# Score and numerator banks exchanged, and layer norm, the head turns and v's projection at other places of a two-layer attention and expert step

## What is computed

```python
x = x + tanh(g_xattn[0]) * xattn0(layernorm(x), ctx, ctx)      # causal mask, 16 heads
x = x + tanh(g_ffn[0])   * moe0(layernorm(x))                  # 8 experts 256->256, top 2, and one shared expert
x = x + tanh(g_xattn[1]) * xattn1(layernorm(x), ctx, ctx)      # masked by length, 16 heads
x = x + tanh(g_ffn[1])   * moe1(layernorm(x))                  # 8 experts 256->1024, top 2

# xattn: q = x @ Wq.T, k = ctx @ Wk.T, v = ctx @ Wv.T
#        probs = softmax(q k^T / 4 + mask);  out = (probs @ v) @ Wo.T
```

## Time and profile before

| | us |
|---|---|
| median of three runs (1742.0, 1742.06, 1753.56) | 1742.06 |
| the profiled execution | 1747.6 |
| its span, first to last instruction | 1745.9 |
| PE busy, DVE busy, ACT busy, POOL busy | 1392.2, 1112.2, 793.0, 727.3 |

### The profile page before, as it was taken

One profiled execution on the slowest core, in us unless ns is written; L12 is line 12 of the kernel. 1 busy time (PEld: TensorE's weight loads), 2 busy tenths in 40 slices (PEclk: granted clock), 3 DMA queues, 4 the chain that ended last, 5 costly groups with the idle time before them and its releaser, 6 DMA issues. The chain is left out here.

```text
span 1745.9 us, 39897 instructions
## 1 busy us (share of the span) xinstructions
PE 1392.2 (80%) x12001; PEld 1176.9 (67%) x12002; DVE 1112.2 (64%) x3589; ACT 793.0 (45%) x1744; POOL 727.3 (42%) x630
## 2 busy tenths in 40 slices
PE   3798988888872777735888887878736999999997
PEld 3576767677651677734556555655426999999997
DVE  4588787877663455523788888887645555555543
ACT  2354545555430555532455455554422544544543
POOL 4334444444231366643344444443232344445422
PEclk9899999999985899975899999999977999999998
DMA  2333334333216677651333333332263324334322
GB/s 88 100 97 100 103 93 110 100 98 88 80 44 185 130 122 131 103 98 55 102 106 102 110 99 109 99 106 65 66 181 105 89 45 96 90 90 96 91 42 42
DMA packets 213629, 168.26 MB, mean 96 GB/s; under 512 B 21462, under 2 KB 207096, under 8 KB 213240
## 3 DMA queue, kind: packets, MB, share of 16 engines
q1 hardware_dynamic: 181112, 126.05, 26.3%
q0 software_dynamic: 26880, 35.80, 12.1%
q10 hardware_dynamic: 5504, 4.75, 1.0%
HBM read 63.80 MB, written 51.56 MB: 66 GB/s over the span
## 5 line engine op out<-in xcount | busy, mean ns | idle before, releaser
L1806 POOL DMA_INDIRECT out_rows<-e_y,e_token x68 | 110.5, 1625 | 235.6 <-DVE e_y L1862 215.8
L1888 ACT ACTIVATE e_h<-e_h,t_up_bias 128x256 f32<-128x256 f32 x272 | 110.5, 444 | 209.0 <-PE e_h L1924 209.0
L938 DVE TENSOR_REDUCE a_row_max<-a_scores 128x2 f32<-128x512 f32 x256 | 170.7, 680 | 41.5 <-PE a_scores L1579 39.9
L1268 ACT ACTIVATE s_w_rows<-a_scores_t 128x384 f32<-128x384 f32 (+1 forms) x256 | 137.7, 547 | 109.9 <-PE a_scores_t L1597 59.9
L1268 ACT ACTIVATE a_probs<-a_scores_t 128x384 f32<-128x384 f32 (+1 forms) x256 | 136.0, 546 | 108.0 <-PE a_scores_t L1597 58.3
L771 POOL DMA_INDIRECT routed_rows_dram<-r_rows,r_slot x128 | 128.3, 1003 | 94.0 <-issue 60.5
L1939 PE MATMUL e_y_bank<-e_down_hi,e_hidden_hi 128*128 128x256 f32 x544 | 157.9, 290 | 3.2 <-DVE e_hidden_lo L1835 3.2
L1924 PE MATMUL e_h<-e_xs_hi,e_up_hi 128*128 128x256 f32 x544 | 154.6, 284 | 3.7 <-DVE e_xs_lo L1827 3.5
L2097 POOL DMA_INDIRECT x_mid_dram<-l_y,l_token x76 | 119.0, 1565 | 86.7 <-ACT l_token L2191 48.5
L1924 PE MATMUL e_h<-e_xs_lo,e_up_hi 128*128 128x256 f32 x544 | 153.8, 283 | 0.0
L1939 PE MATMUL e_y_bank<-s_k_stack,e_hidden_hi 128*128 128x256 f32 x544 | 153.6, 282 | 0.0
(11 more groups left out here) (288 smaller groups left out, 4450.3 us busy)
## 6 DMA issues: line engine op xcount, KB each, us to landing
s_q_stack<-a_parts SPq DMA_DIRECT2D x384, 64.0 KB
s_k_stack<-a_parts SPq DMA_DIRECT2D x384, 64.0 KB
l_xs_rows<-routed_rows_dram SPq DMA_DIRECT2D x42, 258.0 KB
e_xs_rows<-routed_rows_dram SPq DMA_DIRECT2D x36, 258.0 KB
a_ctx_rows<-in_ctx SPq DMA_DIRECT2D x32, 256.0 KB, 3.2
t_up<-in_L_ffn_W SPq DMA_DIRECT2D x8, 1024.0 KB
t_down<-in_L_ffn_W SPq DMA_DIRECT2D x8, 1024.0 KB
routed_rows_dram<-pad_rows ACTq DMA_DIRECT2D x16, 258.0 KB, 9.9
```

Of the source, the lines that this page charges most:

```text
L938: nc.vector.reduce_max(row_max[:, :, h], bank[:].rearrange("p (c t) -> p c t", c=TC), AX_X).then_inc(maxed, 1)
L1268: nc.scalar.activation(probs[h % NP][:, 0:width], scores_t[h % 2][:, 0:width], ACT.Exp).then_inc(probs_ready, 1)
L1806: pool.indirect_dma_start(out=x_acc, out_offset=bass.IndirectOffsetOnAxis(ap=token[p][:, c:c + 1], axis=0), in_=y[p][:, c, :], in_offset=N ...
L1888: nc.scalar.activation(out, h_bank[g][:, at:at + TS], act_func, bias=routed.up_bias[:, bass.ds(e * FC + fc, 1)]).then_inc(hidden_ready, 1)
```

## The change

It does five things.

1. `SB = 3` score banks instead of two: `score_head` waits for the maxima of head h-3. The bank comes from the numerators: one `pv` bank. `mix_group` g=0 and g=2 therefore wait for the `turn_heads` just before, not for the one of an item earlier.
2. Layer norm on DVE: `ln_apply` goes from h=14 to the head of the next step (it is item `i+3` there), `ln_stats` from h=11 to the head of the step, `ln_mean` from h=12 to h=3. POOL's addition of the output bias to x (`bias_of`, layer zero alone) goes from the end of `rstd_of` to the head of POOL's next step.
3. The turning of the heads: `turn_heads` m=0 from h=14 to h=11, `scale_heads` from h=15 to 12, `turn_back` from 15 to 13. Of m=1, `turn_heads` stays at the head, `scale_heads` and `turn_back` go behind the maxima of heads 1 and 2.
4. `project_v` from h=6 to h=11, behind the ranks, with a wait for `counted`; `turn_ctx` from 12 to 13, its `turned_lo` on DVE from 13 to 14. v is copied out of PSUM on ACT in both layers (before: DVE in layer one).
5. `index_to_float` and `mark_chosen` from h=6 to h=8 in layer one (`MARK_AT`); in layer zero they stay at 5.

```diff
+    SB = 3
...
-        scores = [ctx.enter_context(nc.psum_tensor(f"a{layer}_scores{n}", [P, 512], F32)) for n in range(2)]
+        scores = [ctx.enter_context(nc.psum_tensor(f"a{layer}_scores{n}", [P, 512], F32)) for n in range(SB)]
...
-        pv = [ctx.enter_context(nc.psum_tensor(f"a{layer}_pv{n}", [P, 512], F32)) for n in range(2)]
+        pv = ctx.enter_context(nc.psum_tensor(f"a{layer}_pv", [P, 512], F32))
...
-        GATE_AT, O_AT, V_AT, RANK_AT, CTX_AT = (1 if soft else 2, 4, 6, 9, 12)
+        GATE_AT, O_AT, V_AT, RANK_AT, CTX_AT = (1 if soft else 2, 4, 11, 9, 13)
+        MARK_AT = 5 if soft else 8
...
@@ POOL step
+                if causal and i.has(3):
+                    bias_of(i.at(3))
...
@@ DVE step
+                if i.has(3) and i.at(3) > 0:
+                    ln_apply(i.at(3), i.par(3))
                 if i.has(-1):
                     turn_heads(i, -1, 1)
-                    scale_heads(i, -1, 1)
-                    turn_back(i, -1, 1)
+                if i.has(4):
+                    ln_stats(i.at(4), i.half(4), i.par(4))
...
+                    if h == 3 and i.has(4):
+                        ln_mean(i.at(4))
+                    if h == 1 and i.has(-1):
+                        scale_heads(i, -1, 1)
+                    if h == 2 and i.has(-1):
+                        turn_back(i, -1, 1)
...
-                    if h == GATE_AT + 4 and i.has(-2):
+                    if h == MARK_AT and i.has(-2):
                         index_to_float(i)
...
-                    if not causal and h == V_AT + 1 and i.has(1):
-                        evac_v(i)
...
-                    if h == 11 and i.has(4):
-                        ln_stats(i.at(4), i.half(4), i.par(4))
+                    if h == 11 and i.has(0):
+                        turn_heads(i, 0, 0)
...
+                    if h == 12 and i.has(0):
+                        scale_heads(i, 0, 0)
+                    if h == 13 and i.has(0):
+                        turn_back(i, 0, 0)
...
-                    if h == 14 and i.has(0):
-                        turn_heads(i, 0, 0)
-                    if h == 14 and i.has(4):
-                        ln_apply(i.at(4), i.par(4))
-                    if h == 15 and i.has(0):
-                        scale_heads(i, 0, 0)
-                        turn_back(i, 0, 0)
@@ ACT step
-                    if causal and h == V_AT + 1 and i.has(1):
+                    if h == V_AT + 1 and i.has(1):
                         evac_v(i)
@@ PE
             def project_v(i):
...
+                need(pe, counted, i.upto(-2))
                 project(stage[1], 2, ctx_t[i.par(1)], v_done)
             def rank(i):
-                need(pe, v_ready, i.upto(1))
+                need(pe, v_ready, i.upto(0))
             def score_head(i, h):
-                need(pe, maxed, b * H + h - 1)
-                bank, q, k = scores[h % 2], q_stack[p], k_stack[p]
+                need(pe, maxed, b * H + h + 1 - SB)
+                bank, q, k = scores[(b * H + h) % SB], q_stack[p], k_stack[p]
             def mix_group(i, d, g):
                 if g % 2 == 0:
-                    need(pe, heads_turned, (b - 1) * 2 + g // 2 + 1)
-                bank, half = pv[g // 2], g % 2
+                    need(pe, heads_turned, b * 2 + g // 2)
+                half = g % 2
```

More of the change, by code:

```diff
@@ L694, in rstd_of, with bias_of @@
                 nc.gpsimd.tensor_tensor(rstd[:], var_eps[:], minus_half[:], ALU.pow).then_inc(rstd_done, 1)
[L695 to L700 removed]
+            def bias_of(b):
+                pool.wait_ge(xn_ready, b + 1)
+                if b == 0:
+                    pool.wait_ge(bo_gated, 1)
+                nc.gpsimd.tensor_tensor(x_rows(b), x_rows(b), bo_rows[:].unsqueeze(1).to_broadcast((P, TC, D)), ALU.add).then_inc(x_biased, 1)
             rstd_of(0)
@@ L929, in row_maxima @@
                 dve.wait_ge(scores_done, i.at(1) * H + h + 1)
-                bank = scores[h % 2]
+                bank = scores[(i.at(1) * H + h) % SB]
                 if causal:
@@ L1082, in step @@
                 for h in range(H):
-                    if h == 12 and i.has(4):
+                    if h == 3 and i.has(4):
                         dve.wait_ge(stats_done, i.at(4) + 1)
@@ L1614, in mix_group @@
                         at = (t * H + h) * VW
-                        last = nc.tensor.matmul(bank[n * VW:(n + 1) * VW, half * S + first:half * S + S], v_ones[p][:, at:at + VW],
+                        last = nc.tensor.matmul(pv[n * VW:(n + 1) * VW, half * S + first:half * S + S], v_ones[p][:, at:at + VW],
                                                 probs[h % NP][:, col:col + S - first], start=(half == 0 and t == 0),
```

15 lines of the change are left out of this document (1 added, 14 removed).

## The result

The changed kernel took 1720.47 us (median of five, 1709.61 to 1724.55), the kernel before 1749.33 us (five, 1742.0 to 1753.56) beside it: ratio **0.9838, 95% interval 0.9809 to 0.9867**, faster by 1.6%. The forecast was 1704 us in a range of 1680 to 1735. The profiled execution of the changed kernel was the shortest of its five, 1709.61 us (span 1707.9); the sum of the prediction was made against the profiled one of before (1747.6, span 1745.9) and said 38 us less. The spans differ by 38.0 us, the medians by 28.9. So the total lies in the range, but the way to it was another.

What follows compares the result with a forecast made beforehand. Each step was taken as bound by a loop in which PE and DVE wait for each other. Layer one's 34 us and layer zero's 4 made 38 us off the median of 1742.06: 1704 us, range 1680 to 1735.

Steps and rivals of the forecast that it cites:

- Layer one, 31 us: Layer one's full steps: 25.5 us each for 28.3, over 11 steps 31 us less.
- PE sets the end, at 25.5 us: Layer one's step: PE's 22.77 us of work plus waits, 0.9 exponential, 1.1 v, 0.7 ranks and elsewhere; DVE done at 24.4.
- the first rival: k's product behind an idle PE: its slow restart goes too, 0.9 us a step in each layer; 1680 us, 15%.
- Layer zero, 3 us: Layer zero's ten steps: 28.4 us each plus 5 for the clock, 289 for 291.9 us, 3 us less.
- The chain through `shared_down`: Layer zero: `shared_down` waits for context's low part, now behind head 14; the step takes 28.4 us for 28.06.
- the 10.0 us from `turn_max_late` to head 5: Layer zero: PE's k, gate, shared expert's first product and Wo's until DVE takes head 5's maxima, kept at 10.0 us.
- The ramps, 3 and 1 us: Shorter steps before and behind the full ones: 3 us less in layer one, 1 us in layer zero.
- The conversion, 0.86 us: Expert numbers' conversion on DVE in layer one, moved to head 8: 0.86 us for 1.86, partly beside POOL's mask.
- v's new wait, 1.1 us: PE at head 11: v's projection waits about 1.1 us for `counted`, set by DVE behind head 10's maxima.
- One numerator bank, nothing: PE's group behind head 13 waits for `turn_heads`: priced at nothing, otherwise 0.7 us per hand-over, twice a step.
- the second rival: The single numerator bank binds: two hand-overs a step cost PE 0.7 us each; 1733 us, 19%.
- The clock: PE's waits ahead of v's projection and `shared_down` each draw a half-clock stretch in layer zero, one in layer one; 1768 us, 8%.

Runs made afterwards that it cites:

- Q: One of three chips, with four follow-up runs; the kernel before took 1701.29 us there and the changed kernel wasn't run.
- S: One of three chips, with four follow-up runs; the kernel before took 1757.98 us there, the changed kernel 1731.54.
- e9: The kernel of e1 with DVE weighing the rows at head 11 instead of 13, so row transfers are issued earlier: 1712.35 us, 0.9708 of before.
- R: One of three chips, with four follow-up runs; the kernel before took 1752.39 us there, the changed kernel 1725.34.
- e2: The changed kernel with POOL's four row transfers issued a step later, between its two subtractions: 1732.63 us, 1.0184 of before.
- e4: The changed kernel with v's projection back at head 6, without its wait for `counted`: 1688.38 us, 0.9888 of before.
- e3: The changed kernel with two score banks and two numerator banks as before, all moves kept: 1670.38 us, 0.9834 of before.
- e10: The kernel of e1 with the layer norm's work put back where the kernel before has it: 1737.47 us, 0.9894 of before.
- e5: The kernel before with only the layer norm's work moved to the head of the step: 1762.65 us, 1.0059 of before.
- e1: The changed kernel with the early maxima's copy ahead of the context's on ACT: 1653.24 us, 0.9722 of before.

## Why the prediction came out, and where it failed

- **Layer one, 31 us: failed.** The step that failed is "PE sets the end, at 25.5 us", 22.77 us of work and 2.7 of waits. Ten steps of the profile after, from the second update of x on, took 28.7 each: 23.6 of work and 4.9 of waits. The three waits that it counted are there, smaller in sum, 2.0 us (0.3 for the exponential, 1.3 at v, 0.45 at the ranks). What it put at nothing is 0.94 us ahead of `turn_route`, 0.99 ahead of Wo's projection and 0.92 ahead of `project_k`, the first from ACT's order, the others from late completions. The work was also taken from one step at the full clock; its eleven steps have 23.2 us on the mean before and 23.5 after the earlier trace rows, with their stretches at 1.2 GHz, which I had counted in layer zero alone. The walk comes near where nothing completes late: 26.2 us on Q even with two score banks and ACT's order, 25.4 with three and that order mended. The same kernel on S takes 3.5 us more (25.4 against 28.8), 3.1 of it PE's waits, above all for the turned heads and the exponentials. I had seen the sign: k came 2.9 us behind the start of its product, and the first rival put it to "PE's slow restart". It fits the transfers instead. Before, they begin 3.4 us ahead of `turn_max_late`; k's product ends 0.4 us behind the last of them by its rows and its completion comes 0.89 us later, which is the microsecond that I had put to the restart. On Q, where nothing is late beside them, DVE takes the last group at once, and in e9, where they lie elsewhere, k is on time. In the change k's lag went only to return on the last numerator group and on q.
- **Layer zero, 3 us: too little.** The chain through `shared_down` was priced at 28.4 us a step with 5 us for the clock; it gave 279.46 us for ten, 27.95 each. Most of the chain was sized right: from head 5 to the end of the context's low part 14.0 us (14.1 forecast), from there to `turn_max_late` 4.5 (4.3). The term that was wrong is the 10.0 us from `turn_max_late` to head 5, kept from before, with half a microsecond for the clock: it measured 9.6 on the mean, and 8.8 to 9.0 in most steps. The new wait ahead of `shared_down` is there, 0.59 us ended by the context's low part, and the one ahead of v, 1.1 us as forecast; the 0.94 us ahead of `turn_route`, in every step, was not. What I left out was on the side of gain, and it sat in those 10.0 us: the transfers began 1.7 us ahead of `turn_max_late` before, and their late completions hit k, gate and three heads in a row, on R some 10 us a step when added up over PE's rows. Now they begin 4.8 us ahead, and the sum is some 2 us in a full step. On Q, where nothing is late, the same piece takes 8.8 us in all nine steps that I measured.
- **The ramps, 3 and 1 us: too little.** Layer one's last steps gave 13. There completions had been 3.6 to 3.9 us late, with the clock at 0.88 to 0.89 behind the idle time; after the change the same two steps have 1.00:

```profile
1184.10:1216.00 31.90, 25.52 (x203) 17.99 (x202) 23.12 (x62) 15.30 (x32) 11.40 (x11) 0.89 0.28 76
1216.00:1245.20 29.20, 20.40 (x171) 13.33 (x170) 20.85 (x60) 11.51 (x27) 6.90 (x8) 0.88 0.30 83
```

```profile
1159.30:1186.70 27.40, 22.43 (x202) 16.18 (x200) 20.82 (x61) 15.13 (x33) 11.06 (x10) 1.00 0.32 89
1186.70:1209.20 22.50, 18.59 (x171) 12.50 (x170) 18.82 (x58) 11.76 (x30) 7.64 (x8) 1.00 0.39 108
```

- **The conversion, 0.86 us: it took 0.16.** Head 8 is clear of POOL; the bound from layer zero's row held, my walk did not. e2 shows the price of meeting POOL there, 2.75 us.
- **v's new wait, 1.1 us: 1.3 in layer one**, ended by `place_rows` as said. v on ACT took its 0.6 us at no cost that a row shows.
- **One numerator bank, nothing: right** (0.2 us of waiting in the whole trace), so the second rival fell. By what Perfetto Trace Analysis of the Trainium skill, Matmuls, asks of rotating banks the exchange should have cost; e4's wait shows that price, 1.24 us, once v stands elsewhere. The third score bank did end the waits for score banks, which e3 has again at 1.1 us a step of layer one; what their end is worth in time stays open, as said at e3.
- **The clock** rival fell for this change: 0.98 and 0.97 in the windows, where before had 0.96 and 0.98. It is what e4 and e10 show in layer zero, 0.92 over the ten steps of each.

The sum was right by luck, through two errors of opposite sign: 34 forecast and 12 found in layer one with its ramp, 4 forecast and 20 found in layer zero, and 4 to 5 us more ahead of its first update. That the spans differ by just 38 us owes something to the profiled execution, 10.9 us below its kernel's median; by the medians of the three pairs the change gave 28.9, 27.1 and 26.4 us.

## What to carry to other kernels

When a piece of work is moved to another place in a hand-written order, look at the queue of every engine that serves it: here one copy placed ahead of another on ACT, an engine half idle, cost 1.5% of the whole. Don't price such a mend by the wait that it removes: in layer one's full steps the 0.94 us came back elsewhere. Where a consumer starts long after its producer's row ends, ask which other engine is busy over just that stretch, before calling it a slow start; and when a change shifts such work, find what now lies under it. A change of several parts should be tried with each part taken out of the whole, since the parts alone (e5) can have the other sign.

## What the runs showed of the hardware

- While POOL issues its four indirect DMAs of routed rows (about 4.9 us), PE's semaphores come late on two of three chips, 0.8 to 2.2 us on the mean of a layer phase and up to 4.0, and several arrive together about 1.0 to 1.4 us behind the last of them; outside it is about 0.1 us or less. On the third chip 0.02 to 0.16 inside, and the kernel before is 3% faster there (1701 against 1752 and 1758 us). Not every indirect DMA does it: beside the 144 of the expert phases the mean is 0.2 to 0.3 us on R and S and in the first pair, 0.01 on Q. That comparisons must be made on one chip follows: e1's layer one differs by 3.5 us a step between chips, more than any edit but e2's moved it.
- A DVE comparison of 0.19 us took 2.75 us and ended with a POOL subtraction of 2.13 us that began 0.56 us behind it; at its start POOL was still issuing a transfer (e2). Before the change a conversion of 0.16 us took 1.86 beside that subtraction and ended with it. Advanced Engine Details and Errata of the Trainium skill, VectorE Performance Modes, has GpSimd and VectorE's two-port instructions block each other at a shared port; the trace agrees for the conversion. The comparison is a tensor_tensor, for which that section's table gives no two-port mode, and it was held all the same (e2).
